# Handing the events of a max pass to the steps of an attention by their columns instead of evenly

## The reference, cut to what matters

```
L0: att = einsum(q, k) / sqrt(16);  causal mask;                softmax;  ctx = att @ v   (4 heads share one k, v)
L1: att = einsum(q, k) / sqrt(16);  mask by pages of 64 tokens; softmax;  ctx = att @ v
```

## Time and profile before

| | us |
|---|---|
| median of 3 runs | 5369.58 (5366.04 to 5403.41) |
| the profiled execution | 5346.55 |
| its span | 5345.0 |
| attention `B_`, first exponential to last | 198.8 to 1034.7 |
| attention `G_`, first exponential to last | 2449.9 to 3348.0 |

### The profile page before, as it was taken

One profiled execution on the slowest core, in us unless ns is written; L12 is line 12 of the kernel. 1 busy time (PEld: TensorE's weight loads), 2 busy tenths in 40 slices (PEclk: granted clock), 3 DMA queues, 4 the chain that ended last, 5 costly groups with the idle time before them and its releaser, 6 DMA issues. The chain is left out here.

```text
span 5345.0 us, 83726 instructions
## 1 busy us (share of the span) xinstructions
PE 4235.1 (79%) x25572; PEld 2744.0 (51%) x25572; DVE 3021.0 (57%) x5338; ACT 2491.8 (47%) x4463; POOL 1338.6 (25%) x1864
## 2 busy tenths in 40 slices
PE   4899999744889894649989899467896967699687
PEld 2444444243878874324444444255565755566566
DVE  1777878442444442638777686376564436656354
ACT  1477777512454441215666677133453433355343
POOL 1222322123000003110112110133784003378300
PEclk9689989876999997867888898688998989899889
DMA  7212312122121112361223330333552013445211
GB/s 223 35 32 32 53 30 32 62 93 92 48 73 55 48 46 78 113 137 29 41 44 51 53 55 12 125 113 114 163 154 85 32 47 111 144 146 157 71 36 36
DMA packets 327118, 413.95 MB, mean 77 GB/s; under 512 B 40772, under 2 KB 236225, under 8 KB 323196
## 3 DMA queue, kind: packets, MB, share of 16 engines
q1 hardware_dynamic: 278620, 257.43, 15.4%
q0 software_dynamic: 43552, 148.12, 13.1%
q10 hardware_dynamic: 4608, 4.20, 0.2%
HBM read 252.57 MB, written 156.19 MB: 76 GB/s over the span
## 5 line engine op out<-in xcount | busy, mean ns | idle before, releaser
L579 DVE TENSOR_REDUCE G_mpart<-G_pm 128x1 f32<-128x512 f32 (+3 forms) x1024 | 616.9, 652 | 252.6 <-PE G_pm L470 248.5
L579 DVE TENSOR_REDUCE B_mpart<-B_pm 128x1 f32<-128x512 f32 (+3 forms) x1024 | 614.9, 652 | 180.7 <-PE B_pm L470 177.2
L559 ACT ACTIVATE G_p<-G_psc 128x1024 f32<-128x1024 f32 (+3 forms) x640 | 538.1, 896 | 205.7 <-PE G_psc L507 204.1
L559 ACT ACTIVATE B_p<-B_psc 128x1024 f32<-128x1024 f32 (+3 forms) x640 | 537.6, 896 | 151.0 <-PE B_psc L507 149.5
L470 PE MATMUL G_pm<-G_ks,G_qs 48*128 48x512 f32 (+3 forms) x1664 | 485.4, 428 | 80.9 <-DMA G_ks<-G_one 58.8
L470 PE MATMUL B_pm<-B_ks,B_qs 48*128 48x512 f32 (+3 forms) x1664 | 474.4, 415 | 64.1 <-DMA B_ks<-B_one 41.9
L470 PEld LDWEIGHTS G_pm<-G_ks,G_qs 48*128 48x128 f32 x1664 | 268.3, 216 | 418.1 <-DVE G_mpart L579 213.9
L1764 POOL TENSOR_SCALAR J_pr<-J_pr,J_rc 128x256 f32<-128x256 f32 x512 | 463.6, 917 | 40.3 <-DVE J_rc L1902 37.9
L470 PEld LDWEIGHTS B_pm<-B_ks,B_qs 48*128 48x128 f32 x1664 | 259.3, 207 | 393.1 <-DVE B_mpart L579 211.3
L507 PE MATMUL G_psc<-G_qs,G_ks 50*128 50x512 f32 (+3 forms) x1280 | 336.9, 441 | 43.3 <-DMA G_qs<-G_mrow 29.7
L485 PE MATMUL G_po<-G_p,G_v 128*32 128x512 f32 (+3 forms) x2560 | 339.6, 607 | 0.7 <-POOL G_p L341 0.3
(11 more groups left out here) (303 smaller groups left out, 7828.2 us busy)
## 6 DMA issues: line engine op xcount, KB each, us to landing
J_v<-lve SPq DMA_DIRECT2D x64, 520.0 KB, 3.8
J_k<-lkT SPq DMA_DIRECT2D x64, 512.0 KB
lve<-I_v SPq DMA_DIRECT2D x64, 260.0 KB, 2.1
lqT<-I_tT SPq DMA_DIRECT2D x64, 256.0 KB, 2.4
lkT<-I_tT SPq DMA_DIRECT2D x64, 256.0 KB, 2.6
J_q<-lqT SPq DMA_DIRECT2D x64, 256.0 KB
ein<-Z_z SPq DMA_DIRECT2D x8, 1228.0 KB
E_xin<-ein POOLq DMA_DIRECT2D x8, 1152.0 KB, 6.4
```

What stands on the lines that cost most here:

```text
L559: act.activation(p[:, t % 2, 2 * pr:2 * pr + 2, off:CH], psc[:, 2 * pr:2 * pr + 2, off:CH], ACT.Exp, scale=SC).then_inc(e_done[pr], 1)
L579: dve.tensor_reduce(mpart[:, heads[0] % 2, a:z, qb, kc], pm[slots[e]][:, 0:len(heads) * w].rearrange("p (h k) -> p h k", k=w), AX, ALU.max ...
```

## The change

`cut` is no longer even. Each step gets a weight of 0.8 (`FIXED`) plus its width w, and the events are dealt out in proportion; the lead over the steps is 0.57 of an iteration (`LEAD`) instead of 22 steps.

```
-    AHEAD = 22
+    FIXED, LEAD = 0.8, 0.57
...
-    cut = [NE * (t + AHEAD) // NS for t in range(NS + 1)]
+    done = [0]
+    for qc, kb in steps:
+        done.append(done[-1] + FIXED + min(SUB, SUB * (qc + 1) - kb))
+    cut = [round(NE * (d / done[-1] + LEAD)) for d in done]
```

## The result

| | before | after |
|---|---|---|
| median of 20 runs each, same chip | 5371.49 us (5330.27 to 5403.41) | 5388.99 us (5361.23 to 5414.46) |
| ratio, 95% interval | 1 | 1.0041 (1.0023 to 1.0058) |
| profiled execution | 5346.55 us, span 5345.0, clock 0.868 | 5393.5 us, span 5392.0, clock 0.869 |
| `B_`, first exponential to end of the last | 835.9 us | 895.3 us |
| `G_`, the same | 898.1 us | 871.1 us |

The kernel became 0.41% slower, some 22 us. That lies within the 1% held likeliest, and the time within the range. But the forecast said 27 us faster and the sign is wrong.

What follows compares the result with a forecast made beforehand. No engine alone was taken as the bound: PE stands between DVE and ACT. Steps +11, opening +4, clock falls -30 and starts -12 gave -27 us, a median of 5342 us; range 5285 to 5415.

Steps and rivals of the forecast that it cites:

- the 1% held likeliest: Whole kernel: a result within 1%, 54 us, of no change, given a chance of 0.60.
- What bounds the kernel: Inside an attention: no engine is the bound by itself; PE stands between consumers DVE and ACT, in program order.
- Rival 4: Whole kernel: PE is the bound, as its busy row says, so no change, 5370 us; chance 0.05.
- The rule of the steps: Each step lasts the largest of DVE work, ACT work (each plus a wait) and a floor; +11 us over 14 iterations.
- a full-clock iteration off 102 us by more than 2.5: Sign that the forecast is wrong: a full-clock iteration differing from 102 us by over 2.5 either way.
- Opening: Before the first exponential: 84 instead of 81 events, 1.8 us longer in each attention, +3.6 us in all.
- The wait for the row: In `G_`, PE's 29.7 us wait in 5 iterations for chunk 2's row of maxima stays.
- The clock: Half clock from about step 25: three quarters of the falls go, -30 us, bounds 0 and -40.
- The step's own test: Steps 22 and 23: together near 3.4 us, where DVE has gaps, if the forecast is right.
- Rival 3: Clock falls in new places, after steps 1 or 9, or fast starts turn slow: +91 us, 5461; chance 0.12.
- the starts: Steps 0 to 6: two of the four slow starts not following the loop's jump may go, -12 us.
- rival 1: Steps 24 to 28: the clock falls as before, leaving +15 us, 5385; chance 0.18.

Runs made afterwards that it cites:

- e7: Kernel before the change, with each event's matmuls of steps 22, 23 and 24 issued twice; 0.9953 of the kernel before, 5335.89 us.
- e18: Kernel before the change, with event matmuls issued twice in steps 39, 0, 1, 22, 23 and 24; 0.9895 of the kernel before, 5325.54 us.
- e5: Proportional hand-out shifted back so that 81 events are ahead, as in the kernel before; 1.0056 of the kernel before.
- e1: Changed hand-out in attention `B_` alone, `G_` as in the kernel before; 1.0086 of the kernel before, 5405.33 us.
- e3: Changed kernel with POOL's split of a fold moved behind the next step's `clear` and cuts; 1.0009 of the kernel before, 5355.62 us.
- e16: Kernel before, with POOL waiting at step 4 for chunk 2's row before issuing the next heads' loads; 1.0079 of the kernel before, 5414.73 us.
- e10: Kernel before, with POOL issuing the next heads' loads at step 6 instead of 4; 1.0005 of the kernel before, 5346.2 us.

## Why the prediction was wrong

**What bounds the kernel** was right: PE between two consumers. Rival 4 (PE bound by its busy row) is out: e7 and e18 give PE some 200 and 400 more matmuls and the kernel gets faster.

**The rule of the steps** had the sign right and the size wrong. This is the larger of the two failed steps: "+11 us" measured +33 in the profile. By stretch, at full clock, `B_`, predicted change against measured: steps 0 to 4 -1.2, -1.1; 5 to 7 +0.6, +1.1; 8 to 12 0, -0.9; 13 to 16 +0.9, +1.1; 17 to 24 -1.9, +0.7; 25 and 26 +1.8, -0.2; 27 to 35 +2.6, +3.7; 36 to 38 -1.1, 0; step 39 -1.0, -1.1. The terms that missed are the ones that were to return time: steps 17 to 24 and 36 to 38 gave nothing. Half of that was in the prediction's own list. For steps 36 to 38 it has 8.2 before, 7.1 after and 7.2 measured before; they measured 7.2 after too. The rule was right for the new order and 1 us too high for the old, where DVE-full narrow steps were evened out by their neighbours. Over the iteration it says 103.2 before and 104.0 after, against 99.6 and then 102.9 and 101.0. So the sentence that failed is "I trust its difference more than its sum": the 4% by which the rule was high did not carry over to the new order, and the gain it saw there was a gain over a time that the kernel never took. The sign "a full-clock iteration off 102 us by more than 2.5" couldn't show this, since the iteration before was 99.6 us, not 102.

In step 17 the ACT row shows why: "2.94 us on ACT" is only its work, and a block's matmuls stand behind `weigh`, so 1.3 us of waiting come on top. Step 25, the other with two blocks, took 2.95 us, near the rule's 3.04, and step 26, priced at over 3.3 with its five events, took 2.12; that is why 25 and 26 came out 2 us under the rule. The time came back in steps 27 and 28, 7.1 us where the rule says 5.7. What parts step 25 from step 17 is read from one stretch of each, above; no experiment moved it. Of steps 17 to 24, 0.9 us in `B_` is the wait for POOL (below), which `G_` doesn't have. How much of the rest the missed wait accounts for isn't shown; it is read from step 17 (1.2 us) and argued for the others.

**Opening**: the term was too small. From DVE's first piece to the first exponential the opening of `B_` took 49.75 us before and 52.86 after, that of `G_` 49.75 and 52.87: +3.1 us each, not +1.8. The three events are not all of it: in e5, with 81 ahead as before, the opening takes 51.38 us, so the new order of the events costs there too. **The wait for the row**: stays, 29.7 to 28.6, as said.

**The clock** is the other failed step: "three quarters of the falls go: -30 us". The price of a fall was right (40 us for 14, and e7 got 39.6). That PE is sparse ahead of the falls is shown by steps 22 to 24 beside e7, not by the earlier trace rows, which the prediction cites and which begins at step 24. In `G_` all 7 went. In `B_` 6 of 7 stayed (4 in e1). The sentence that failed is "POOL's folds come one step earlier, before a `clear` that is not yet due": the `clear` of step 22 was due, `B_`'s masks take 0.64 us each, and PE stood 1.19 us before the `weigh` of step 22. e3 takes this away and all but one of the falls go. The step's own test, that steps 22 and 23 come to 3.4 us together, fails in `B_` (1.29 + 2.75 or more) and is met in `G_` (1.15 + 1.93).

**Rival 3**, given 0.12, happened in part: the new falls it named, after steps 8 and 9, came after step 12, in 6 of 7 iterations of `B_` (15.5 us) and in all 7 of `G_`, where 5 already had one behind the wait for the row. It did not take the starts: these cost 20 us less than before, near the -12 of the forecast. That the change did this isn't shown: in e7, with the same instructions at the starts as before, all 7 iterations of `B_` started slow instead of 4. The whole came out between the forecast and rival 3. That it is near rival 1's 5385 is luck: rival 1's condition, that the falls stay, held in 6 of 14 places, and its price of the steps was a third of the measured one.

In the terms of the sum: +11 + 4 - 30 - 12 = -27 forecast; in the profile +33 + 6 - 12 - 20, plus +23 and +10 of falls and waits elsewhere that had no term. That is 40 of the 47 us between the two profiles; the last iterations (-2) and the program outside of the attentions (+9) are the rest.

## What to carry to other kernels

Two loops woven into one instruction stream are ruled less by how many items each step gets than by where the special ones meet: here blocks that another engine must copy right behind five pieces, a fold on an in-order queue ahead of a mask, and a row beside bulk loads. So list these meetings step by step for the new order, each with the wait in front of it and not only its work, and measure the neighbours of the lead (three events moved this kernel by 1.4 to 2.2%) before crediting a scheme. Where half clock follows a sparse stretch of TensorE, repeated matmuls whose result is already there are a cheap test of what the clock costs, and here the best version.

## What the runs showed that I had not expected

- More work made it faster: issuing the event matmuls of six of 40 steps twice gave 0.9895 (0.9844 to 0.9947), of three 0.9953.
- PE counts as busy for 20.68 of 20.68 us in a stretch at clock 0.50 and 13.79 of 14.64 at 1.00: in these rows the busy share is highest where the clock is lowest, so a high share is no sign that PE does more.
- A row of maxima of 16 KB, issued by SP about 4 us after POOL's first loads of the next heads, was complete 27 us after the step's start; issued ahead of the loads (e16), after 5.3 us.
- A transfer written two steps later in POOL's program was issued at nearly the same moment as before (e10).
- Moving `weigh` by one or two events took the changed kernel from 1.0041 to 1.0443, ten times what the whole change cost.
